# A mixture-of-experts block on one core: the dispatch of a chunk on GpSimd waits for the next chunk's feed-forward input

## The reference, cut to what matters

```python
# L0: adapter by domain
hidden = gelu(x @ down_W.T + down_b)
x = layernorm((expert(hidden) + domain_emb[idx]) @ up_W.T + up_b + x) * gamma + beta
# L1: attention block with adaptive norm, 16 heads, and a feed-forward
x = _ln(x) * (1 + scale) + shift
x = x + (attention(x, attention_bias, mask) @ Wo + bo)
h = _ln(x) * g2 + beta2
x = x + _gelu2(h @ W1 + b1) @ W2 + b2
# L2: a rotation of neighbouring features by two angles
# L3: norm, style by subject, then top 2 of 8 experts for each token
gates, idx = top_k(softmax(h_flat @ router_w), 2)
hid = relu(einsum('nd,edf->nef', h_flat, exp_w1) + exp_b1)
y = einsum('ned,ne->nd', einsum('nef,efd->ned', hid, exp_w2) + exp_b2, combine)
return x + y
```

## Time and profile before

| what | value |
| --- | --- |
| time, median of 3 runs | 747.1 us (745.82 to 747.19) |
| the profiled execution's own time | 752.83 us |
| its span in the profile | 751.0 us |
| TensorE busy | 576.8 us (77%) |
| VectorE busy | 484.2 us (64%) |
| GpSimd busy | 271.4 us (36%) |
| ScalarE busy | 262.0 us (35%) |
| mean granted clock of TensorE | 0.864 |

### The profile page before, as it was taken

One profiled execution on the slowest core, in us unless ns is written; L12 is line 12 of the kernel. 1 busy time (PEld: TensorE's weight loads), 2 busy tenths in 40 slices (PEclk: granted clock), 3 DMA queues, 4 the chain that ended last, 5 costly groups with the idle time before them and its releaser, 6 DMA issues.

```text
span 751.0 us, 16208 instructions
## 1 busy us (share of the span) xinstructions
PE 576.8 (77%) x5068; PEld 432.0 (58%) x5069; DVE 484.2 (64%) x1306; ACT 262.0 (35%) x548; POOL 271.4 (36%) x200
## 2 busy tenths in 40 slices
PE   3518587996979877769576963439999999999992
PEld 1416384583864756638474452327778777777771
DVE  5673785899789798626987136715656565656661
ACT  1215534425343253143332301004444444443440
POOL 0731728167055370327803220400323333323332
PEclk9559699999888999779885895559999999999997
DMA  8622473130325323174132567465222222222320
GB/s 287 231 81 78 147 254 140 36 114 0 113 99 211 134 92 113 44 266 166 59 113 78 175 238 261 181 242 168 48 43 47 42 43 39 42 45 34 49 42 1
DMA packets 41144, 86.28 MB, mean 115 GB/s; under 512 B 7317, under 2 KB 31790, under 8 KB 37006
## 3 DMA queue, kind: packets, MB, share of 16 engines
q1 hardware_dynamic: 22896, 65.13, 24.9%
q0 software_dynamic: 7200, 8.60, 6.7%
q10 hardware_dynamic: 11006, 12.01, 5.2%
HBM read 57.18 MB, written 29.44 MB: 115 GB/s over the span
## 4 chain that ended last, share of the span: by engine, by line
PE 49%; DVE 22%; issue 9%; DMA 7%; ACT 4%; ACTq 3%; POOL 3%; another core or an unknown queue 1%; POOLq 0%; SPq 0%; DVEq 0%
PE bank L1740 7%; PE bank L1562 6%; PE bank L1729 4%; PE bank L1731 4%; PE bank L1730 4%; DMA out_x<-x_kept,ids 4%; PE bank L1571 4%; PE bank L1741 3%; PE bank L1459 2%; DMA stage<-in_moe_w 2%; PE bank L1526 2%; PE bank L1542 2%; DVE stats L953 2%; PE bank L1516 2%; DVE w_moe L1076 2%
## 5 line engine op out<-in xcount | busy, mean ns | idle before, releaser
L1729 PE MATMUL bank<-xs_f,w_moe 128*128 128x128 f16 x624 | 123.9, 221 | 7.2 <-issue 5.7
L1731 PE MATMUL bank<-xs_f,w_moe 128*128 128x128 f16 x624 | 123.9, 221 | 0.0
L1730 PE MATMUL bank<-xs_f,w_moe 128*128 128x128 f16 x624 | 123.4, 221 | 0.0
L831 ACT ACTIVATE stage<-bank,cols 128x128 f32<-128x128 f32 x312 | 88.6, 376 | 95.6 <-PE bank L1731 82.9
L1729 PEld LDWEIGHTS bank<-xs_f,w_moe 128*128 x624 | 61.4, 98 | 43.1 <-issue 14.4
L629 POOL DMA_INDIRECT out_x<-x_kept,ids x39 | 62.0, 1590 | 64.4 <-DVE x_kept L1379 34.4
L1740 PE MATMUL bank<-w_moe,split 128*128 x208 | 78.6, 380 | 0.9
L573 POOL DMA_INDIRECT dispatched<-disp,slot x32 | 34.6, 1080 | 119.4 <-DVE disp L1166 55.6
L1562 PE MATMUL bank<-w_moe 128*128 128x512 f32 x128 | 63.0, 655 | 9.9 <-ACT w_moe L707 9.9
L1730 PEld LDWEIGHTS bank<-xs_f,w_moe 128*128 x624 | 61.6, 99 | 2.6
L920 DVE SCALAR_TENSOR_TENSOR split<-stage,split 128x2048 f16<-128x2048 f32 x16 | 39.9, 2494 | 35.2 <-ACT split L657 35.2
(11 more groups left out here) (242 smaller groups left out, 1248.1 us busy)
## 6 DMA issues: line engine op xcount, KB each, us to landing
stage<-in_moe_w SPq DMA_DIRECT2D x16, 1024.0 KB, 8.4
w_split<-split SPq DMA_DIRECT2D x16, 1024.0 KB, 4.9
w_moe<-w_split SPq DMA_DIRECT2D x8, 2048.0 KB, 8.1
w_moe<-in_bias SPq DMA_DIRECT2D x8, 1024.0 KB, 10.5
xs<-dispatched ACTq DMA_DIRECT2D x41, 130.0 KB
w_moe<-in_x_f SPq DMA_DIRECT2D x4, 512.0 KB, 5.8
w_moe<-in_x_t SPq DMA_DIRECT2D x4, 512.0 KB, 5.0
out_x<-x4b ACTq DMA_DIRECT2D x4, 512.0 KB
```

Source lines behind the costliest of these rows:

```text
L831: ins = act.activation(h32[j][:, f, :], bank[2 * j + g][:, P * (f % 4):P * (f % 4) + P], ACT.Relu, bias=moe_b1[:, bass.ds(e, 1), f], scale ...
L1729: pe.matmul(o, hi, xs_f[j][:, k, :], start=(k == 0), stop=False)
L1730: pe.matmul(o, hi, xs_f[j][:, KD + k, :], start=False, stop=False)
L1731: mm = pe.matmul(o, lo, xs_f[j][:, k, :], start=False, stop=(k == KD - 1))
```

## The change

`dispatch(c)` gets one more wait, for all chunks but the last: both halves of the next chunk's feed-forward input must have been written before its first indirect DMA is issued.

```diff
                 pool.wait_ge(slot_ready.sem, slot_ready.of(c, 1))
                 pool.wait_ge(disp_ready.sem, disp_ready.of(c, 1))
                 pool.wait_ge(rows_ready.sem, rows_ready.of(c, 2))
+                if c + 1 < NCH:
+                    pool.wait_ge(h_ready.sem, h_ready.of(c + 1, 2))
                 pool.nop(nofuse=True)
                 for i in range(TT):
                     for a in range(2):
```

## The result

The change is slower. The median of 20 runs is 753.5 us (746.7 to 758.1), against 746.5 us (744.8 to 748.9) for 20 runs of the kernel before beside them: a difference of 7.0 us. The ratio, 1.0086 with a 95% interval of 1.0068 to 1.0105, is worked out from the fast runs alone, without the change's slowest one, and so isn't the quotient of the two medians. The forecast was 741.3, its range ended at 749.5. The profiled execution of the change took 751.95 us, its span 750.1.

A forecast was written before the change was run, and what follows sets the result against it. TensorE's work was about half the chain; waits while GpSimd issued dispatches were removable. Profiled: 5.5 + 6.5 - 0.5 = 11.5 us; plain: 3.0 + 3.3 - 0.5 = 5.8, so 747.1 to 741.3, range 735.5 to 749.5.

The forecast's parts named there:

- Step (c): Chunk 1's moved dispatch: chunk 3's mask 3.0 us later, no root steps beside it; cost 0.5 us, at most 3.0.
- The slower rival: Chunk 2's mask directly follows the residual, slowing VectorE's root steps: 2.1 us lost, 749.2 us; chance 0.23.
- the late completions: TensorE work finishing later than modelled while GpSimd issued early dispatches, seen as unknown waits of 2.19 and 7.31 us.
- Step (b): Chunk 0's moved dispatch: bias lands at 236.2, root steps run quickly; 5.5 us gained, 2.2 from the wait, 3.3 otherwise.
- the 1.8 us window for the root steps: GpSimd still from 234.4 to 236.2, between residual and chunk 2's mask, letting VectorE's nine inverse-root operations run quickly.
- the port: Less GpSimd work beside VectorE's root steps in pass 1, called the quieter port: 3.3 us of gain.
- Step (a): Unexplained waits before the feed-forward input of chunks 0 and 1 go: up to 3.2 and 6.5 us, at least nothing.
- The rival that the waits have another cause: The unexplained waits stay despite the moved dispatches, leaving only 3.3 us gain and 0.5 cost: 744.3 us; chance 0.21.
- Step (d): Chunk 2's moved dispatch, from 411.4 to 422, with no bias loaded any more: no effect.

The follow-up runs named there:

- e8: The kernel before, unchanged, profiled a second time: 748.5 us, span 746.6.
- e1: The change with only chunk 1's dispatch waiting for the feed-forward input: 755.5 us, ratio 1.0115 to the kernel before.
- e5: The change with the second four of chunk 3's eight mask adds waiting for VectorE's split: 749.4 us, ratio 1.0039 to the kernel before.
- e3: The change with the masks of chunks 2 and 3 waiting for VectorE's split: 741.3 us, ratio 0.9927 to the kernel before.
- e11: The change with chunk 3's mask alone waiting for VectorE's split: 747.5 us, ratio 0.9908 to the kernel before.
- e6: The kernel before with an extra 1 MB HBM-to-HBM DMA ahead of the bias loads of chunks 2 and 3: 746.3 us, ratio 0.9987.
- e4: The kernel before, dispatches unmoved, with the masks of chunks 2 and 3 waiting for VectorE's split: 743.7 us, ratio 0.996.
- e12: The change run again, beside the kernel before at its higher level of 753.0 us: 754.4 us, ratio 1.0017.
- e9: The change with an empty GpSimd instruction ahead of each mask add: 750.3 us, ratio 0.9947 to the kernel before.
- e2: The change with only chunk 0's dispatch waiting for the feed-forward input: 745.5 us, ratio 0.9992 to the kernel before.
- e14: The change with the masks of chunks 2 and 3 behind the split, run again beside the kernel before at 753.0 us: 741.1 us, ratio 0.984.
- e10: The change with only chunk 2's dispatch waiting for the feed-forward input: 753.1 us, ratio 0.9994 to the kernel before.
- e13: Only chunk 0's dispatch waits and chunk 2's mask follows the split, run again beside the kernel before at 753.0 us: 748.2 us, ratio 0.9922.
- e15: The kernel before, unchanged, profiled on an occasion at its higher level: median 753.0 us.
- e7: The change with only chunk 0's dispatch waiting, and chunk 2's mask behind VectorE's split: 739.6 us, ratio 0.9908 to the kernel before.

## Why the prediction was wrong, by its steps

**Step (c) failed, and it decided the time.** It said that beside chunk 3's mask there are no root steps, and priced the earlier mask at 0.5 us, 3.0 if covers go. It looked for small operations on VectorE and passed over a large one, `split_low` L920 (128x2048, from `stage` and `split`), which stands there in every trace. In the kernel before it takes 2.28 to 2.39 us, because GpSimd has stood still for the bias (13.57 us in the earlier trace rows, 5.83 in e8) when it arrives. The moved dispatch filled that idle time, so residual and mask became one run, and the split lost to the whole of it: 13.59 us instead of 2.36, and pass 2 is 8.0 us longer. The step's own working had a gap that would have let the split in, residual done at 331 and the mask from 332.3; it rested on the bias being 3.0 us late, and in the change there was no gap. e1 (all of the loss), e5 (half the adds, a third of the loss), e3 and e11 (order changed, loss gone) and e6 (traffic added, no blocked split and 2.4 us in that pass) agree on this. With the order changed pass 2 takes 88.8 to 88.9 us and not 86.3; e4 shows the same in the kernel before, so that rest is the gate's price.

**The slower rival named the right mechanism in the wrong pass.** "The mask comes straight behind the residual" happened in pass 1 too. There the chain of the change reads

```profile
231.71 1.38 DVE var L941
233.11 1.21 DVE rstd L942
234.34 1.20 DVE newton L944
...
241.66 1.20 DVE rstd L950
```

with all nine steps slow, and the rival priced that at 2.1 us. It cost nothing in this trace, since without the late completions the kernel before has nearly the same (seven slow steps in e8): in e8 the mask starts 15.28 us behind chunk 1's L707 (236.13 - 220.85), in the change 15.35 (233.02 - 217.67), and turn1 starts 26.87 and 26.73 behind it. The earlier trace rows come from an execution with the late completions, where four steps escaped.

**Step (b) failed in the change, though what it counted on does happen.** The bias was not put off by 3.0 us to 236.2. It had landed by 233.0, when the mask began directly behind the residual, and in pass 2 by 329.6. In this trace the 1.8 us window for the root steps never opened, and the 3.3 us of gain with it. In other traces with dispatch 0 moved GpSimd did stand still ahead of the mask, for 0.3 us (e11, e12), 0.8 (e9) and 1.8 (e2). In e2 the last eight steps were quick, and pass 1 took 94.2 us. That the window is worth something was right: e4 opens it with a wait of its own, e6 by the late bias, and pass 1 falls from 98.8 to 92.9 in both. How often it opens in the plain runs isn't known; e2's spread of 10.9 us leaves room for it. No run shows the port to which the step puts down 3.3 of its 5.5 us; the runs show root steps of 1.15 to 1.20 us each beside the adds and of 0.16 or 0.17 ahead of the mask (e6). The whole of the change's pass 1 is 1.4 us shorter than e8's. Turn1 accounts for 0.14; the rest comes later in the pass. TensorE's granted clock was 0.93 in the third quarter against 0.86 in e8; whether that is the reason isn't shown.

**Step (a) was right in that the waits go when the dispatches move, and near in size, but the waits were absent from the runs it was applied to.** The unknown waits disappear wherever dispatches 0 and 1 wait, and appear only where one of them is early: never in the change, e3, e5, e9, e11, e12, e14; in the first profile, e10, e13, e15. But the kernel before has them only on some occasions. Its runs beside the change, at 746.5, agree with a kernel without them (e8), and the 753 level with one that has them (e15); no plain run has a trace, so this is an inference from the levels. The text kept 3.0 us of 8.7 in its sum; there was nothing to keep. Where they exist, between e15 and e12 pass 0 falls by 3.4 us and pass 1 by 5.0, where the step had 3.2 and 6.5. On those occasions taking them away gives back what the split costs: 1.0017. With the split's cost mended as well, e14 gains 11.9 us. That is near the 11.5 of the prediction's full sum, and e3's 741.3 us is the forecast itself, but both are chance: those kernels have waits ahead of the masks that the change hasn't, and quick root steps by them.

In sum, for plain runs the prediction had 5.8 us of gain and the runs showed 7.0 of loss. Of these 12.8 us, 3.0 are waits that weren't there, 3.3 the window less 1.4 that pass 1 gained otherwise, and 7.5 the split (8.0 where 0.5 was allowed); that is 12.4.

The rival that the waits have another cause would have had the change leave them. On the occasions that have them the runs speak against that reading: TensorE's completions came up to 7.3 us late beside an early dispatch (7.25 us in e13 and e15, 5.68 in e10) and were on time in every trace without one. How the dispatch delays them isn't shown.

**Step (d) was right.** With the wait for chunk 2 alone the ratio is 0.9994 (e10).

**What the split waited for.** In e8 it waited for one running add at most, and took 2.36 us. An estimate from that for the split in the change is what was left of the residual, 1.7 us, and perhaps one add of 1.24. It waited for nine instructions, 11.4 us. In e1, e5, e9 and e12 too (11.99, 6.04, 13.59 and 10.87 us) it ended 2.15 or 2.16 us behind the last add that stood ready.

## What to carry to other kernels

A wait that delays one item of an engine's queue can also remove the idle gaps behind it (here the 5.83 us of e8 ahead of chunk 3's mask): list what now stands back to back there, and look on the other engine for every long instruction in that stretch (here the split, 13.59 us instead of 2.36), not only for the small ones. Where one is found, order the two by a semaphore, the run of short operations behind the long one that it would hold up: here a wait ahead of two masks turned +7 us into -5 (e3, 741 us at either level of the kernel before, and so the version to use; e7 is faster, 739.6, on one of them only). Where the profiled execution is slower than the plain runs, as here by 5.7 us, an odd wait in its trace may not be theirs at all: profile once more before pricing it.

## What the runs showed of the hardware that was not expected

- VectorE's 128x2048 split (L920), 2.28 us alone, lost to a gapless run of GpSimd's adds in five traces out of five where the mask came straight behind the residual (13.59, 13.59, 11.99, 10.87, and 6.04 to four adds). Where GpSimd had stood still before the mask, it got in at the next add, at most 0.4 us late in pass 2 (2.29 to 2.70 in the first profile, e7, e8, e10, e13, e15) and 1.1 us in pass 1 (3.35 in e2 and e6). A run without a gap is not enough to hold it out: in pass 1 of e3 and e4 the split arrived during GpSimd's L536 (3.6 us), between the mask and L526 with no gap on either side, and waited for that one operation only (4.97 and 5.19 us). There GpSimd had stood still before the mask. Small operations of 128x4 beside the adds get in one at each add in either case, 1.2 us each instead of 0.17. What decides who wins is open.
- GpSimd's indirect DMA of 128 rows takes 0.96 us and 0.30 to the next; with the split (L920) beside them single ones took 2.1 to 3.4 us (2.13 and 3.38 in e8).
- TensorE's completions came 0.7 (e10) to 7.3 us (the first profile) late beside an early dispatch, on two of the five occasions of timed runs and in the first profile; why only then is open.
